# A graph network on one core: node rows copied and made elsewhere, round 4 and Chebyshev parts rearranged

## The reference

```python
x = _layernorm(x + _L0_gnn_ref(x, ...))   # attention over edges, five hops
x = _layernorm(x + _L1_gnn_ref(x, ...))   # four rounds of a normalized sum over neighbours
x = _layernorm(x + _L2_gnn_ref(x, ...))   # Chebyshev: two passes over the edges
x = _layernorm(x + _L3_gnn_ref(x, ...))   # one aggregation and two products
# L0: softmax over the edges of a source of leaky_relu(s_h + s_t + s_r), A = 0.9 * att, and five times
msgs = A[:, :, None] * Z[tail_ids]
Z_new = segment_sum(msgs, head_ids) + 0.1 * Z0
# L1: each round
h = x @ W; msgs = h[src] * norm[:, None]
agg = segment_sum(msgs, dst) + b
x = (agg - mu) * rsqrt(var + EPS) * gamma + beta
# L2
Tx1 = prop(x); Tx2 = 2.0 * prop(Tx1) - x; out = x @ W[0] + Tx1 @ W[1] + Tx2 @ W[2] + bias
```

## Time and profile before

| | |
|---|---|
| median of three runs | 10144.71 us |
| the profiled execution | 10132.72 us, span 10130.9 us |
| busy PE / DVE / ACT / POOL | 5679.1 / 6629.9 / 3121.4 / 7119.2 us |
| mean granted clock of PE | 0.711 of full |
| HBM read / written | 852.84 / 795.02 MB |

### The profile page before, as it was taken

How to read it: one execution, slowest core, us unless ns; L and a number is a source line. 1 busy time by engine, 2 the same in 40 slices (tenths; PEclk the granted TensorE clock), 3 DMA queues, 4 the chain that set the end, 5 groups by cost and what they waited for, 6 DMA issues and landing times. The chain is left out here.

```text
span 10130.9 us, 117410 instructions
## 1 busy us (share of the span) xinstructions
PE 5679.1 (56%) x28423; PEld 4053.3 (40%) x28423; DVE 6629.9 (65%) x13576; ACT 3121.4 (31%) x5997; POOL 7119.2 (70%) x7145
## 2 busy tenths in 40 slices
PE   3856999500000001777777786767764769833338
PEld 1453333100000001765656565555553658733336
DVE  8954333387878786886767786877775767622227
ACT  2542222163222222543434342322221432200006
POOL 2564777677777777777777676767776767677764
PEclk9978999755555555887878897777776775555559
DMA  0074333265545454447867676655444984311127
GB/s 14 4 239 133 73 70 73 41 204 159 166 146 165 146 165 139 139 124 198 223 213 227 213 261 201 232 159 146 134 136 135 334 265 131 106 47 46 46 64 279
DMA packets 1256874, 1519.23 MB, mean 150 GB/s; under 512 B 835537, under 2 KB 956719, under 8 KB 1256634
## 3 DMA queue, kind: packets, MB, share of 16 engines
q1 hardware_dynamic: 995656, 1253.98, 38.0%
q0 software_dynamic: 252192, 248.44, 11.2%
q10 hardware_dynamic: 8786, 14.21, 0.4%
HBM read 852.84 MB, written 795.02 MB: 163 GB/s over the span
## 5 line engine op out<-in xcount | busy, mean ns | idle before, releaser
L2978 POOL DMA_INDIRECT r_got<-state,comb_src x1176 | 1140.4, 970 | 367.0 <-issue 345.0
L336 POOL DMA_INDIRECT payload_or_bias_rows<-payload,place x784 | 782.4, 998 | 474.0 <-issue 253.0
L1949 PE MATMUL hop_ps_into<-hop_out,span_s 128*128 128x256 f32 x8 | 4.9, 713 | 1865.2 <-DVE hop_out L1759 1865.2
L1540 POOL DMA_INDIRECT hop_got<-edges_a,next_col x784 | 782.6, 998 | 259.2 <-issue 238.4
L1949 PEld LDWEIGHTS hop_ps_into<-hop_out,span_s 128*128 128x128 f32 x8 | 2.0, 311 | 1865.7 <-DVE hop_out L1759 1865.7
L3257 PE MATMUL r_ps_v<-dense1g,r_gt 128*128 128x128 f32 x4312 | 747.1, 341 | 0.0
L3257 PEld LDWEIGHTS r_ps_v<-dense1g,r_gt 128*128 128x128 f32 x4312 | 675.9, 246 | 159.7 <-issue 159.7
L3138 DVE TENSOR_REDUCE r_stat<-r_sq 128x14 f32<-128x896 f32 x448 | 483.8, 1080 | 258.7 <-ACT r_sq L3311 256.9
L1838 ACT COPY hop_got<-hop_zeros 128x1792 f32<-128x1792 f32 x168 | 283.0, 1684 | 1083.0 <-DVE hop_ps_msg L1704 1083.0
L3083 DVE SCALAR_TENSOR_TENSOR r_acc<-r_acc,r_runs_now,r_got 128x64 f32<-128x64 f32 (+1 forms) x1564 | 447.2, 286 | 255.4 <-DMA r_got<-state,comb_src 199.5
L1759 DVE SCALAR_TENSOR_TENSOR hop_out<-hop_out,hop_runs_now,hop_ps_msg 128x256 f32<-128x256 f32 x1176 | 565.5, 481 | 50.9
(11 more groups left out here) (782 smaller groups left out, 17727.9 us busy)
## 6 DMA issues: line engine op xcount, KB each, us to landing
state<-r_y SPq DMA_DIRECT2D x252, 448.0 KB, 2.9
r_in<-state SPq DMA_DIRECT2D x252, 448.0 KB, 4.7
edges_a<-hop_out SPq DMA_DIRECT2D x112, 896.0 KB
edges_b<-hop_out SPq DMA_DIRECT2D x112, 896.0 KB, 4.3
hop_side<-x_dst SPq DMA_DIRECT2D x280, 224.0 KB, 4.5
own<-plain_y SPq DMA_DIRECT2D x56, 952.0 KB
g_rows<-r_gx SPq DMA_DIRECT2D x112, 448.0 KB, 2.5
x_and_sums<-c_y SPq DMA_DIRECT2D x56, 896.0 KB
```

The costliest lines, as they stand in the source:

```text
L336: nc.gpsimd.indirect_dma_start(out=t.raw[:, n, :], out_offset=None, in_=t.pay[k], in_offset=bass.IndirectOffsetOnAxis(t.place[:, k, n:n + ...
L1540: pool.indirect_dma_start(out=got[:, u, c, :], out_offset=None, in_=table, in_offset=at, bounds_check=EP - 1, oob_is_err=False).then_inc(g ...
L2978: pool.indirect_dma_start(out=got[:, n, c - b * CT, :], out_offset=None, in_=table, in_offset=bass.IndirectOffsetOnAxis(idx[:, at + c:at + ...
```

## The change

It does five things.

1. `plain_rows` is removed. The x part of the table is written by 33 copies within memory (`place_inputs`, SP): 8 pieces beside the sort, 25 beside the histogram, two under way. Of the node's row only the marks are stored later (`store_marks`, SP and ACT, four DMAs each). `EARLY` becomes 250 and `UNDER_DEGREES` 272. The clears move from ACT to SP. `edge_scores` gathers 68 in place of 65 numbers of the target and stores zeros into half of the rows of `x3a`.
2. The products X1 of the nodes are made in hops 1 and 2, one tile of 7 x 128 nodes beside each step.
3. In round 4 the inverse is kept in PSUM, in the spare columns of `ps_g`.
4. `cheb_first` merges its two inputs on PE by 14 accumulating matmuls with the identity in place of 7 transposes; the edge work moves to lag 4.
5. `cheb_first` loads and stores only 64 of 128 (or 65) numbers of a node's row.

```diff
-EARLY = 208
-UNDER_DEGREES = 222
+EARLY = 250
+UNDER_DEGREES = 272
+X_PIECES = 16
+X_UNDER_SORT = 8
+MARK_PIECES = 8
...
+def place_inputs(sp, t, x, first, last):
+    given = x.rearrange("(p j) w -> p j w", p=P)
+    places = t.nodes1.rearrange("(p j) w -> p j w", p=P)
+    for k in range(first, last):
+        wait(sp, t.x_placed[k % 2], k // 2 * 16)
+        n = k % X_PIECES
+        lo_n, hi_n = n * J // X_PIECES, (n + 1) * J // X_PIECES
+        if k == 2 * X_PIECES:
...
+        elif k >= X_PIECES:
+            sp.dma_start(places[:, lo_n:hi_n, X1], given[:, lo_n:hi_n, :]).then_inc(t.x_placed[k % 2], 16)
+        else:
+            hi_n = min(hi_n, J - 1)
+            with_next = bass.AP(x.tensor, x.offset + lo_n * D, [[J * D, P], [D, hi_n - lo_n], [1, ROW]])
+            sp.dma_start(places[:, lo_n:hi_n, PLAIN:WIDE], with_next).then_inc(t.x_placed[k % 2], 16)
...
+def store_marks(nc, t):
...
+            for n in range(parity, MARK_PIECES, 2):
+                some = slice(n * J // MARK_PIECES, (n + 1) * J // MARK_PIECES)
+                eng.dma_start(places[:, some, MARKS:MARKS + 4], t.marks[:, some, :]).then_inc(stored, 16)
...
+                    sp.dma_start(t.x3a[0:NP, :].rearrange("(p j) w -> p j w", p=P)[:, n * T:(n + 1) * T, D:2 * D],
+                                 no_sums[:]).then_inc(sums_cleared, 16)
...
 (edge_pass, SyncE)
+                        for i, u in ago(0):
+                            sp.dma_start(xin[:, u % 2], w["x"].rearrange("(p j) d -> p j d", p=P)[:, node_columns(i, u), :]).then_inc(xin_in[u], 16)
+                        for i, u in ago(4):
+                            sp.wait_ge(xy_ready[u], i + 1)
+                            sp.dma_start(t.nodes1.rearrange("(p j) w -> p j w", p=P)[:, node_columns(i, u), X1], xy[:, u]).then_inc(xy_kept[u], 16)
 (edge_pass, VectorE, behind the seven running sums)
+                    for i, u in ago(2):
+                        dve.wait_ge(xroot_ready[u], i + 1)
+                        nc.vector.reciprocal(xstat[:, u % 2, 2, :], xstat[:, u % 2, 1, :]).then_inc(xinv_ready[u], 1)
+                    for i, u in ago(1):
+                        dve.wait_ge(xsq_ready[u], i + 1)
+                        nc.vector.tensor_reduce(xstat[:, u % 2, 0, :], xsq[:, u % 2], AX.X, ALU.add).then_inc(xsum_ready[u], 1)
 (edge_pass, ScalarE, ahead of the copy of runs)
+                    for i, u in ago(2):
+                        act.wait_ge(xsum_ready[u], i + 1)
+                        nc.scalar.activation(xstat[:, u % 2, 1, :], xstat[:, u % 2, 0, :], ACT.Sqrt, scale=1.0 / D, bias=eps[:]).then_inc(xroot_ready[u], 1)
...
+                    inverse = ps_g[:, k, TD:TD + T] if tjoin else rstat[:, k, 3, :]
...
-                    nc.vector.scalar_tensor_tensor(result(i, u)[:, :, 0:D], r[:, j_slot(u)], 1.0, per_node(rstat[:, k, 3, :]),
+                    nc.vector.scalar_tensor_tensor(result(i, u)[:, :, 0:D], r[:, j_slot(u)], 1.0, per_node(inverse),
...
-    MERGE, TURN, PROD, NORM, LAST, GRAM = 1, 2, 3, 4, 5, 6
+    TURN, PROD, NORM, LAST, GRAM = 1, 2, 3, 4, 5
+    EDGES = LAST
...
-                    sp.dma_start(put0[:, u], nodes(t.x2, i, u)).then_inc(put0_ok[u], 16)
+                    sp.dma_start(put0[:, u], nodes(t.x2, i, u)[:, :, 0:D]).then_inc(put0_ok[u], 16)
...
-                    sp.dma_start(nodes(t.x3a, i, u), y[:, u % 2]).then_inc(y_stored[u % 2], 16)
+                    sp.dma_start(nodes(t.x3a, i, u)[:, :, 0:D], y[:, u % 2]).then_inc(y_stored[u % 2], 16)
...
-                    nc.vector.tensor_tensor(in0[:, u], in0[:, u], put0[:, u, :, 0:D], ALU.add).then_inc(merged[u % 2], 1)
...
+                        nc.tensor.matmul(ps_t[:, n * P:(n + 1) * P], in0[:, u, 2 * n:2 * n + 2, :].rearrange("p t d -> p (t d)"), t.ident[:],
+                                         start=True, stop=False, skip_group_check=True)
+                        ins = nc.tensor.matmul(ps_t[:, n * P:(n + 1) * P], put0[:, u, 2 * n:2 * n + 2, :].rearrange("p t d -> p (t d)"), t.ident[:],
+                                               start=False, stop=True, skip_group_check=True)
```

More of the change, by code:

```diff
@@ L141, in tensors @@
     t.got_s, t.got_t = (ctx.enter_context(semaphore(nc, n)) for n in ("got_s", "got_t"))
+    t.x_placed = [ctx.enter_context(semaphore(nc, f"x_placed{u}")) for u in range(2)]
     t.in_degree = dram("in_degree", [NP, 1])
@@ L1400, in _, with edge_pass @@
                 c.link(nc.vector.scalar_tensor_tensor(t.att_e[:], e[:], 0.9, tot[:], ALU.mult, ALU.mult))
-def edge_pass(nc, t, name, kind, runs, span, fix, table=None, idx=None, put=None, target=None, after=None, w=None, aside=None):
+def edge_pass(nc, t, name, kind, runs, span, fix, table=None, idx=None, put=None, target=None, after=None, w=None, aside=None, first_node=None):
     heads = kind in ("heads", "heads_out")
@@ L1629, in _ @@
                         sp.wait_ge(y1_kept[u], ROUNDS * 16)
+            if first_node is not None:
+                for u in range(RING):
+                    sp.wait_ge(xy_kept[u], ROUNDS * 16)
             if aside == "weights":
@@ L1826, in _ @@
                                              scale=0.1).then_inc(side_scaled[u], 1)
+                    if first_node is not None:
+                        act.wait_ge(xt_done[u], i + 1)
+                        past(act, xv_done, i, u, 2)
+                        nc.scalar.copy(gx[:, u % 2, 0:3 * P], ps_aside[:, 0:3 * P])
+                        nc.scalar.copy(gx[0:D, u % 2, 3 * P:], ps_aside[0:D, 3 * P:]).then_inc(gx_ready[u], 1)
+                for i, u in ago(0):
                     if begins:
@@ L1847, in _ @@
                                              ACT.Relu).then_inc(msg_ready[u], 1)
+                if first_node is not None:
+                    for i, u in ago(0):
+                        act.wait_ge(xv_done[u], i + 1)
+                        wait(act, xy_kept[u], i * 16)
+                        nc.scalar.copy(xy[:, u].rearrange("p c d -> p (c d)"), ps_into[:, 0:CT * D])
+                        past(act, xsum_ready, i, u, 2)
+                        nc.scalar.activation(xsq[:, u % 2].rearrange("p c d -> p (c d)"), ps_into[:, 0:CT * D], ACT.Square).then_inc(xsq_ready[u], 1)
+                    for i, u in ago(3):
+                        act.wait_ge(xinv_ready[u], i + 1)
+                        for c in range(CT):
+                            ins = nc.scalar.activation(xy[:, u, c, :], xy[:, u, c, :], ACT.Copy, scale=xstat[:, u % 2, 2, c:c + 1])
+                        ins.then_inc(xy_ready[u], 1)
                 if rows_too:
@@ L2283, in _ @@
[L2283 to L2300 removed]
+            pieces(sp, 0)
@@ L2325, in node_degrees @@
+            pieces(act, 1)
 def node_degrees(nc, t):
```

241 lines of the change are left out of this document (104 added, 137 removed).

## The result

The changed kernel took 10013.31 us in the median of four runs (10006.11 to 10014.81) beside 10148.01 us for the kernel before: ratio 0.9867, 95% interval 0.985 to 0.9884. The forecast was 10012 us. The profiled execution took 10013.65 us, span 10011.5, which is 119.4 us less than the span before. The total agrees much better than the terms do, so the stages come first. Each row is read from each kernel's own trace: the first three from one first instruction to another, round 4 and the Chebyshev pass from the first to the last instruction of the stage, the last stage to the end of the span.

What follows compares the result with a forecast made beforehand. Stages had different limits (POOL steady, DMA and DVE in places), so each was priced alone: -123 +54 -40 -23 +1 = -131 from 10132.72 gives 10002, plus 12 for the median, taken as 10012; range 9950 to 10085 (own 9985 to 10040).

Steps and rivals of the forecast that it cites:

- The node-row stage, -123: Node-row stage replaced by copies and marks: next stage's first DVE work near 713 instead of 836.39, -123 us.
- The term that I took at 0 there, the marks: Marks stage: 16-byte stores take 55 to 110 us, under the gathers' 154; cost 0 up to 24.6 ns a row.
- The copies cost nothing: 33 copies within memory at 17.6 ns a packet stay hidden under sort and histogram: 0 us, upper bound +118.
- The limits that I gave: Copies lose cover above 36 ns a row in the histogram and some 46 in the sort.
- Rival B: Short rows to memory cost double, 37 ns, in histogram copies and first Chebyshev pass: 10113 us; chance 0.11.
- Hops, +54: Hops 1 and 2 turn from POOL-bound into a DVE-ACT ring, step 9.6 us: +30 and +24, +54 us.
- Round 4, -40: Round 4: inverse in PSUM stops DVE instructions with two SBUF inputs lengthening POOL's: -40 us, bounds -47 and 0.
- 60 ns on 786: Round 4: POOL's mean of 1010 ns against 950 in the second Chebyshev pass, over 786 instructions: 47 us.
- L3116 is harmless: Round 4: the 28 L3116 instructions don't lengthen gathers, so the change gains 47 us, otherwise 35.
- First Chebyshev pass, -23: First Chebyshev pass: POOL's mean gains 14 us, shorter tail 18, DMA set against them: -23, bounds -35 and +64.
- The +9 that I set against them for DMA: First Chebyshev pass: DMA cost of 256-byte-row loads and stores, set against gains of 14 and 18 us.
- Rival C: First Chebyshev pass: PE stays at 1.2 GHz, step 13.4 to 14 us, +211 there: 10246 us; chance 0.07.

Runs made afterwards that it cites:

- the second (711.5): The changed kernel run again unaltered in the third set, beside the kernel before: 9998.09 us, ratio 0.9859; its trace has source_fields starting at 711.5.

## Why the prediction was right, and where it was not

- *The node-row stage, -123.* Right in place and size: -116.0 in the first trace, -124.9 in the second (711.5). The histogram held its 250 gathers (last end 508.7, worked out 508.6) and the marks stage began at 556.0 (worked out 556). The term that I took at 0 there, the marks, came out at its edge: I gave a 16-byte row 9 to 17.6 ns, half and all of a 252-byte load, and said that above 24.6 the stores set the end; they take 21.4 to 24.5 ns. The 24.5 are the first trace's, in which the stage ended 7 us later than forecast.
- *The copies cost nothing.* Right in outcome, wrong in the step: "17.6 ns a packet" was taken from loads into SBUF. A 272-byte row within memory takes 36 to 39 ns of an engine, a 256-byte one 21.6. The limits that I gave (36 ns in the histogram if all pieces cost the same, some 46 in the sort) show how near it was: 39 is above the first, and only the 256-byte pieces saved it. The first limit was too high besides, since the copies start there at 192.4 us, behind SP's loads of the weights, and not at 165: (524 - 192.4) / 9800 is 34 ns. The kernels with all pieces 272 bytes wide and with eleven copies beside the sort pass the two limits and pay. Rival B had too low a chance, and its price was half met: dear rows, but with cover left.
- *Short rows.* The first Chebyshev pass stores its y as 256-byte rows from SBUF and became shorter; in the hops 256-byte rows were stored with no loss in a loop at a DMA share of 0.65. What cost double were 272-byte rows from memory to memory. Below the rate of long rows they are all: in hop 1 a 256-byte packet lasts 18 ns, 14 bytes a ns, and one of 1792 bytes 74 ns, 24 bytes a ns. The Trainium skill (DMA: Bandwidth & Descriptors, section Specifications) has one limit for line rate, 512 bytes. These packets agree with it, and the 67% between 256 and 272 bytes are a step below it.
- *Hops, +54.* The mechanism was right (waits, order and undoing it all agree), the size too large: +37.6. Two terms were mis-sized. The step was 9.52 (mean 9.48, as the first ones run ahead) and not 9.6, which makes 6.7 us a hop. In the step shown the DVE's part is 8.41 us for 8.7, since the reciprocal starts under the last running sum and the reduce under the reciprocal, and ACT's part is 1.11 us for 0.95, since its root takes 0.30 and not 0.21. The tail from the last running sums to the end of POOL's put took 7.1 us, not 9.5: the put waits for the store of those sums to land, 5.4 us after its issue, and not for the scalings, of which seven take 1.77 us and not up to 3.9.
- *Round 4, -40.* The failing step is the base: "60 ns on 786" compared a stage of gathers and puts with one of gathers alone. A put is dearer than a gather to begin with: the last layer has

```profile
L1552 POOL DMA_INDIRECT x_and_sums<-gin_out,put_s x392 | 389.0, 992 | 119.4 <-issue 119.4
```

in the kernel before, and in round 4 the puts beside none of the 84 instructions take 988 ns. Against 992 and 950, round 4's 1050 and 970 hold 23 and 8 us, 31 in all. -23.5 came: 17.4 in the puts and 6.0 in the gathers. With the inverse back in SBUF the stage took 20.8 us back, all of the puts' part and half of the gathers'. That L3116 is harmless, one of my two cases, is out. The Trainium skill (SBUF — State Buffer, section SBUF: two separate sides) has the whole instruction as the length of such a block, and only against GpSimd work that reads SBUF. The trace agrees that two SBUF inputs lengthen POOL's work, with 231 ns in the mean for a put beside an instruction of 1092 ns.
- *First Chebyshev pass, -23.* Measured -31.6: POOL's mean fell nearly as expected (985 to 956 ns, 11 us for 14) and the tail from 30.6 to 10.3 (20 us for 18). The +9 that I set against them for DMA is the term that failed: it didn't bite, although the share is 1.02, since 256-byte packets, y's stores among them, last 18.7 ns there and lasted 18.2 before. Rival C didn't come: PE's clock went from 0.75 to 0.94, with rests before the transposes of 1.7 us in the mean for 4.6.
- *The sum.* The errors of the four terms (measured less forecast) were +7, -16, +17 and -9 us, which cancel by chance. The span still came out 12 us over the forecast for it (-119 for -131), 8 of them in the last stage, where the other runs show scatter. That the median lies within 1 us of the forecast has one more accident in it: I added the 12 us by which the profile of before lay under its median, and the profile of the changed kernel lay at its own. A total within 1 us is not a forecast good to 1 us.

## What to carry to other kernels

When work is laid beside a loop with an idle engine, draw the ring that it closes: a short instruction at the head of one engine's step whose input ends another engine's step costs its whole way round, and moving it behind what the other engine waits for can make it free (here 38 us in two hops for moving one instruction). Price an operation by rows of the same kind: a put by puts, a copy within memory not by loads, and let a hidden transfer's cover be worked out with twice the price before trusting it. If terms of both signs cancel, look at stages, not at the total.

## What the runs showed that I had not expected

- Copies within memory of 272-byte rows (544 apart) take 36 to 39 ns a row and engine, at either offset and with two or four under way; of 256-byte rows, written to offset 0 only, 21.6 ns.
- Stores of 16-byte rows take 21.4 to 24.5 ns each and engine, on one queue or two, in a stage that holds little else; 256-byte packets in hop 1, loads and stores with SBUF, last 18 ns each in the trace.
- A store of 256 KB on the same queue as running copies waits for them (eleven copies beside the sort: 20 us).
- POOL pauses ahead of the 114th payload gather of a stage, 3.2 us with the DMA engines idle (share 0.07), 6.9 in the old node-row stage (0.82) and up to 12.7 beside the stores of the marks, and the DRAIN at the stage's end takes 9.2 us where 112 gathers ran without a pause, 1.6 us where a pause lies seven gathers back. Moving gathers from one stage to another moves these too.
